# A three-layer graph network with a mixture-of-experts stage on one core: the first tiles of the next stage are put ahead of the last kept-back products

## The reference

```python
def _sage_layer(x, src, dst, Wl, bl, Wr, a):
    msg = x[src]
    agg = jax.ops.segment_sum(msg, dst, num_segments=n)
    deg = jax.ops.segment_sum(jnp.ones(...), dst, num_segments=n)
    agg = agg / jnp.maximum(deg, 1.0)[:, None]
    out = agg @ Wl + bl + x @ Wr
    return jnp.where(out >= 0, out, a * out)
...
x = x + three _sage_layers(_layernorm(x))
h = _layernorm(x); probs = softmax(h @ Wr + br); the two largest of 8 stay as cw
x = x + sum over e of cw[:, e] * (relu(h @ W1[e] + b1[e]) @ W2[e] + b2[e])
```

## Time and profile before

| | |
|---|---|
| median of 3 runs | 2694.34 us (2692.85 to 2696.75) |
| the profiled execution | 2695.04 us, its span 2693.4 us |
| PE busy | 2629.3 us, 98% of the span |
| VectorE, ScalarE, GpSimd busy | 1806.5, 1270.8, 992.5 us |
| mean granted clock of TensorE | 0.992 of full speed |

### The profile page before, as it was taken

The page is one execution under the profiler, slowest core; times in us unless marked ns, Lnnn a source line. Parts: engine busy times, 40 slices in busy tenths (PEclk is TensorE's granted clock), DMA queues, the critical chain, the costliest instruction groups (busy, mean ns, idle before and its releaser), DMA issues.

```text
span 2693.4 us, 39731 instructions
## 1 busy us (share of the span) xinstructions
PE 2629.3 (98%) x9195; PEld 1508.0 (56%) x9195; DVE 1806.5 (67%) x5090; ACT 1270.8 (47%) x2681; POOL 992.5 (37%) x1054
## 2 busy tenths in 40 slices
PE   7999999999899999999899999999899999999999
PEld 3444445554588855555488865555455555555554
DVE  5555555554799955555599965555477777777775
ACT  2222245554488855555288855555222222222222
POOL 2222255553344445554233335555222222222221
PEclk9999999999999999999999999999999999999999
DMA  4344378886255568887245558888422222222221
GB/s 133 133 133 132 118 224 271 264 273 224 88 164 164 164 201 269 273 263 259 90 164 164 164 181 268 268 272 264 148 85 86 82 83 90 85 82 83 89 85 48
DMA packets 200943, 446.57 MB, mean 166 GB/s; under 512 B 34383, under 2 KB 34695, under 8 KB 200836
## 3 DMA queue, kind: packets, MB, share of 16 engines
q0 software_dynamic: 64928, 207.55, 26.7%
q10 hardware_dynamic: 69168, 126.12, 12.8%
q1 hardware_dynamic: 66740, 111.54, 11.8%
HBM read 238.50 MB, written 207.11 MB: 165 GB/s over the span
## 4 chain that ended last, share of the span: by engine, by line
PE 95%; DMA 2%; DVE 1%; ACT 1%; issue 1%; SPq 0%; DVEq 0%; POOL 0%; ACTq 0%; POOLq 0%
PE psY L602 11%; PE psY L582 10%; PE psH L582 10%; PE psM L713 9%; PE psY L713 8%; PE psH L713 8%; PE psT L576 6%; PE psY L616 6%; PE psY L624 5%; PE psY L633 5%; PE psS L725 4%; PE psS L726 4%; PE psM L582 2%; PE psH L602 2%; PE psS L576 1%; PE psH L809 1%
## 5 line engine op out<-in xcount | busy, mean ns | idle before, releaser
L510 POOL DMA_INDIRECT rows<-y_rows,lists x471 | 487.3, 1035 | 473.9 <-PE psS L726 313.5
L1186 DVE TENSOR_TENSOR lows<-rows,highs 128x512 fp32r<-128x512 f32 x471 | 326.1, 692 | 374.5 <-ACT highs L842 341.4
L517 POOL DMA_INDIRECT rows<-sum_rows,nodeI x237 | 296.0, 1249 | 338.7 <-DVE rows L1194 305.2
L842 ACT ACTIVATE outs<-psS 128x512 f32<-128x512 f32 x471 | 279.6, 594 | 284.9 <-PE psS L726 251.3
L842 ACT ACTIVATE highs<-rows 128x512 fp32r<-128x512 f32 x471 | 294.6, 625 | 144.1 <-ACT outs L842 98.6
L725 PE MATMUL psS<-highs,sel 128*128 128x512 f32 x471 | 348.8, 740 | 7.3 <-ACT outs L842 7.3
L491 POOL TENSOR_TENSOR st<-st,small 128x1 f32<-128x1 f32 x158 | 90.0, 570 | 663.2 <-DVE st L1086 663.2
L602 PE MATMUL psY<-wy,res 128*128 128x512 f32 x632 | 287.0, 597 | 0.8 <-ACT res L842 0.8
L582 PE MATMUL psY<-wy,xTs 128*128 128x512 f32 x632 | 285.8, 595 | 0.0
L582 PE MATMUL psH<-wz,hTs 128*128 128x512 f32 x632 | 284.2, 592 | 0.7 <-ACT hTs L842 0.7
L713 PE MATMUL psM<-wz,res 128*128 128x512 f32 x544 | 255.4, 592 | 0.0
(11 more groups left out here) (166 smaller groups left out, 4108.9 us busy)
## 6 DMA issues: line engine op xcount, KB each, us to landing
sum_rows<-outs ACTq DMA_DIRECT2D x471, 256.0 KB
y_rows<-outs SPq DMA_DIRECT2D x237, 256.0 KB
rows<-in_x POOLq DMA_DIRECT2D x78, 256.0 KB, 2.9
outs<-in_x SPq DMA_DIRECT2D x78, 256.0 KB
out_rows<-res SPq DMA_DIRECT2D x78, 256.0 KB, 2.0
rows<-y_rows,lists POOLq DMA_INDIRECT x471
rows<-sum_rows,nodeI POOLq DMA_INDIRECT x237
wy<-in_L_gnn_Wl SPq DMA_DIRECT2D x3, 1024.0 KB, 7.2
```

The costliest lines, as they stand in the source:

```text
L510: pool.indirect_dma_start(out=rows[:, t % RING, :], out_offset=None, in_=y_d, in_offset=bass.IndirectOffsetOnAxis(ap=col(srcT, t), axis=0) ...
L517: pool.indirect_dma_start(out=rows[:, s, :], out_offset=None, in_=s_d, in_offset=bass.IndirectOffsetOnAxis(ap=col(nodeI, t), axis=0), boun ...
L842: act.activation(o, i_, ACT.Copy).then_inc(signal, 1)
L1186: dve.tensor_tensor(lows[:, t % RING, :], rows[:, t % RING, :], highs[:, g, :].bitcast(F32), ALU.subtract)\
```

## The change

At the first two changes of stage, PE transposes tiles 0 and 1 of the next layer between k6 and k7, and its wait for all `z_sb` before the second transpose is gone. VectorE makes `next_x` of tiles 0 and 1 behind `take_z` of k5, `bend` and `x_high` of tile 0 (`high_x`, cut out of `split_x`) behind that of k6, and `w_low` between `take_z` of k7 and of k8. ScalarE's first copy waits for `mend_add` (the mended sums added, which frees `psS`) in place of all `z_ps`. At the third, VectorE does both `ahead` calls of the expert stage behind `take_z` of k5, and then takes k6, k7 and k8. PE's list is not changed there. The wait of ScalarE's `norm` is changed in the same way. An unused helper (`edge_blocks`) is gone, and the layer loop of VectorE stands behind the definition of `experts`; line numbers move by this.

```diff
@@ dense (PE)
-                x_transpose(0, 0, k)
-                all_turns(pe, z_sb, k)
-                x_transpose(0, 1, k)
                 pe.wait_ge(high_parts, k)
@@ sum stage (PE)
-                for node in late[2:]:
+                for node in late[2:-2]:
+                    z_product(*node, l)
+                if l + 1 < LAYERS:
+                    x_transpose(0, 0, l + 1)
+                    x_transpose(0, 1, l + 1)
+                for node in late[-2:]:
                     z_product(*node, l)
@@ ScalarE, layers 1 and 2
-                    all_turns(act, z_ps, l)
+                    act.wait_ge(mend_add, 2 * l)
@@ ScalarE, experts
-            all_turns(act, z_ps, LAYERS)
-            act.wait_ge(mend_ps, 2 * LAYERS)
+            act.wait_ge(mend_add, 2 * LAYERS)
@@ split_x (VectorE)
+            def high_x(i, c, k):
+                t, s, n = at(i, c, 2)
+                dve.wait_ge(xT_kept[s], k * uses(s) + n + 1)
+                dve.wait_ge(hh_ps, (k - 1) * NT + t)
+                dve.tensor_scalar(x_high[:, :], kept(t), UNDER, None, ALU.mult).then_inc(xh_set, 1)
+
             def split_x(i, c, k):
                 t, s, n = at(i, c, 2)
                 used = (k - 1) * NT + t
-                dve.wait_ge(xT_kept[s], k * uses(s) + n + 1)
-                dve.wait_ge(hh_ps, used)
-                dve.tensor_scalar(x_high[:, :], kept(t), UNDER, None, ALU.mult).then_inc(xh_set, 1)
+                if not (isinstance(i, int) and i + c == 0):
+                    high_x(i, c, k)
@@ VectorE, end of a layer (the loop stands elsewhere now; only what differs)
-                for node in late[3:]:
-                    take_z(*node, l)
-                if l + 1 < LAYERS:
-                    split_low(l)
-                all_turns(dve, z_sb, l + 1)
-                if l + 1 < LAYERS:
-                    next_x(0, 0, l + 1)
-                    next_x(0, 1, l + 1)
-                    bend(0, 0, l + 1)
-                    each_split(dve, lambda i, c: split_x(i, c, l + 1))
-                else:
-                    dve.wait_ge(avec_in, 16)
...
-            for t in range(2):
-                experts(0, t - 2, numbered(t, AHEAD, done[0]), own=False)
-            done[0] += 2 * AHEAD
+                for node in late[3:-3]:
+                    take_z(*node, l)
+                if l + 1 < LAYERS:
+                    next_x(0, 0, l + 1)
+                    next_x(0, 1, l + 1)
+                    take_z(*late[-3], l)
+                    bend(0, 0, l + 1)
+                    high_x(0, 0, l + 1)
+                    take_z(*late[-2], l)
+                    split_low(l)
+                    take_z(*late[-1], l)
+                else:
+                    dve.wait_ge(avec_in, 16)
+                    for t in range(2):
+                        experts(0, t - 2, numbered(t, AHEAD, done[0]), own=False)
+                    done[0] += 2 * AHEAD
+                    for node in late[-3:]:
+                        take_z(*node, l)
+                all_turns(dve, z_sb, l + 1)
+                if l + 1 < LAYERS:
+                    each_split(dve, lambda i, c: split_x(i, c, l + 1))
```

More of the change, by code:

```diff
@@ L305, in each_four @@
             step(PAIRS, 0)
-        def edge_blocks(eng):
-            yield (0, 1), [(0, 0), (0, 1)]
-            yield (1, 0), [(0, 2), (0, 3)]
-            yield (1, 1), [(1, 0), (1, 1)]
-            for i in span(eng, 2, PAIRS):
-                yield (i, 0), [(i, -2), (i, -1)]
-                yield (i, 1), [(i, 0), (i, 1)]
-            yield (PAIRS, 0), [(PAIRS - 1, 2), (PAIRS - 1, 3), (PAIRS, 0)]
         def landed(t, l):
@@ L1409, in _, with take_edge @@
             AHEAD, OWN = 6, 11
-            for t in range(2):
-                experts(0, t - 2, numbered(t, AHEAD, done[0]), own=False)
-            done[0] += 2 * AHEAD
+            for l in range(LAYERS):
+                if l == 0:
+                    make_plan()
+                dve.wait_ge(bvec_in, 16 * (l + 1))
+                def take_edge(e):
+                    select(*e, l)
+                    low(*e, l)
+                take_z(0, 0, l)
+                take_z(0, 1, l)
+                take_edge((0, 0))
+                take_edge((0, 1))
+                for t in range(2, FIRST):
+                    take_z(t // 2, t % 2, l)
+                for nodes, edges in sum_blocks():
+                    for e in two_on(edges):
+                        take_edge(e)
+                    for node in nodes:
+                        take_z(*node, l)
+                late = late_nodes()
+                take_z(*late[0], l)
+                if l + 1 < LAYERS:
+                    split_high(l)
+                take_z(*late[1], l)
+                for b, r in BLOCKS:
+                    g = MEND_SLOT[b]
+                    dve.wait_ge(mend_g[b], 16 * (l + 1))
+                    dve.wait_ge(mend_ps, 2 * l + b + 1)
+                    dve.tensor_tensor(rows[0:r, g, :], rows[0:r, g, :], psS[b][0:r, :], ALU.add)\
+                       .then_inc(mend_add, 1)
+                take_z(*late[2], l)
+                if l + 1 < LAYERS:
+                    split_cross()
+                for node in late[3:-3]:
+                    take_z(*node, l)
+                if l + 1 < LAYERS:
+                    next_x(0, 0, l + 1)
[12 more added lines that the diff above has]
+                    for node in late[-3:]:
+                        take_z(*node, l)
+                all_turns(dve, z_sb, l + 1)
+                if l + 1 < LAYERS:
+                    each_split(dve, lambda i, c: split_x(i, c, l + 1))
```

32 lines of the change are left out of this document (removed).

## The result

| | before | after |
|---|---|---|
| median, 8 runs each, taken side by side | 2696.18 us (2692.85 to 2697.07) | 2686.88 us (2686.25 to 2688.88) |
| the profiled execution, its span | 2695.04 us, 2693.4 us | 2686.95 us, 2685.2 us |

The ratio is 0.9969, with a 95% interval of 0.9958 to 0.9980. The medians differ by 9.3 us, the two profiled spans by 8.2 us. The forecast was 6.3 us.

What follows compares the result with a forecast made beforehand. PE, busy for 98% of the span, bounds the kernel, so time comes only from its idle or low-clock stretches. 7.1 - 0.8 = 6.3 us off 2695.04 gives 2688.7, median 2688.0; range 2683.5 to 2692.5.

Steps and rivals of the forecast that it cites:

- Transposes ahead of k7 and k8: First two changes of stage: two transposes moved ahead of k7 win 3.5 and 3.6 us, sum 7.1, bounds 6.5 to 7.6.
- So no wait, with a margin of 1.2 and 0.8 us: First two changes of stage: gathers land 3.4 us after issue, so the moved transposes find their input with this margin.
- rival D: Gathers of tiles 0 and 1 land late, PE waits ahead of k7 and its clock falls: slower, 2699.1 or 2701.1; 6%.
- The clock at the first two changes: PE's clock falls again behind k8: booked 0, bounds +1.8 for each change of stage above and -1 below.
- rival B: The clock holds at the first two changes, with one PE wait of 3.6 us: adds 3.6, 2684.4 us; 13%.
- A new wait of 2.7 us: Third change: k8 on PE waits for `take_z` of k6 behind the `ahead` calls, starting at 1942.8 instead of 1940.12.
- The two chances in three: Third change: the wait ahead of k8 may let the clock fall under k8, half of 3.3 us, booked as 1.1 lost.
- `b1` opens the first `own` row 3.3 us sooner: Third change: `b1`, issued at 1947.15, lands 4.3 us later, so VectorE's first `own` row starts at 1951.5.
- I take 1953.8 as the start of L1335: 2.5 us sooner, bounds 1.8 and 3.3: Third change: VectorE's row needing tile 2's `x` rows starts 2.5 us sooner, transfers being through 6.7 us behind first issue.
- PE resumes on the low clock: Third change: PE stands still from about 1953 till 1959.2, then runs on the low clock: 2.2 us lost, bounds 1.2 to 3.0.
- The sum: All three changes of stage: 7.1 us won at the first two, 0.8 lost at the third, 6.3 us won.
- A: The forecast itself, over the whole kernel: 6.3 us won, median 2688.0 us; 60%.

Runs made afterwards that it cites:

- the first experiment: The changed kernel with its third part undone, `take_z` of k6 to k8 ahead of the `ahead` calls again: 2687.28 us, ratio 0.9965.

## Why the prediction was right

**Transposes ahead of k7 and k8.** Right in place and sign. The forecast was 18.6 us from k5 to the third transpose; it is 18.08 at both changes of stage. Three terms were a little too dear. Behind k5's start `w_low` came after 14.92 us, not 15.04, as eight transposes among the products cost 0.88 and not 1.0. The wait for `w_low` was 0.15, not 0.33. And `next_x` of tile 2 followed `take_z` of k8 after 0.72, so the 0.25 for its own `z_sb` was nothing. Together 4.1 won for each (22.14 and 22.18 before), not 3.5 and 3.6.

**"So no wait, with a margin of 1.2 and 0.8 us".** No wait was right, the margin was not. I took 3.4 us from the issue of a gather to its reader. It was 3.68 both times (686.05 to 689.73, 1303.29 to 1306.97). A transpose follows the start of its `next_x` after 0.85, and tile 1's begins 0.5 behind the start of the eight, at 691.34 and 1308.09. That leaves margins of about 0.8 and 0.3 us. The experiment one place earlier shows the other side of this edge: rival D's mechanism, a late `next_x` ahead of a transpose and a lower clock behind it, is real. Only part of the delay was the gathers' there, and by the profiles the two changes of stage lost 6.1 us.

**The clock at the first two changes.** I booked 0, with 1.8 each as the bound. In the profiled execution it fell at the second and not at the first, and the first gave 1.5 more (5.54 in place of 4.06). That was rival B in one of two places. Which way it goes isn't settled by the program: the idle time was 3.20 at both, and the profile of the first experiment has the low clock at both, with 25.20 and 26.37 us to the transpose of tile 4. Six profiles have this order and this idle time: the clock fell behind it in three of six at the first change and in six of six at the second. No row tells what decides it. So the 1.5 us are a chance of about one in two that came out well in this execution.

**"A new wait of 2.7 us" ahead of k8.** It is 2.34, and k8 starts 2.5 later behind k5 than before. The two chances in three that the clock falls under it (1.1 us) were not paid in the changed kernel's profile. They were in that of the moved `b1` wait, where k8 took 5.40: 1.7 us, as priced. Six kernels have this wait of 2.34 or 2.35, and the clock fell under k8 in that one alone, so the chance was put too high.

**`b1` opens the first `own` row 3.3 us sooner.** It did: 21.58 us behind k5, against 24.98 before, so 3.4.

**"I take 1953.8 as the start of L1335: 2.5 us sooner, bounds 1.8 and 3.3".** This is the step that failed. It was 1.3 us sooner (25.14 behind k5 instead of 26.45), outside my bounds. I had let the transfers be through 6.7 us behind the first issue, as in the kernel before; it took 7.88 (1937.42 to 1945.30). In the kernel before, nobody had waited for these rows, so 6.7 rested on a DMA share in a window and not on a reader. And it was another burst. First the `x` rows' issues in the kernel before (tile 2 at 1948.5, tile 3 at 1952.4), then those of tiles 2 and 3 in the changed kernel with the time to landing, and the same in the kernel that issues them first:

```profile
L370 SPq DMA_DIRECT2D outs<-in_x x2: 327/328/328, 1948.5 to 1952.4; - x2
...
outs<-in_x SPq DMA_DIRECT2D x2, 256.0 KB, 7.0
...
outs<-in_x SPq DMA_DIRECT2D x2, 256.0 KB, 2.6
```

Before, tile 2's rows went out 4.0 us behind `b1`, and tile 3's only when all was through. In the changed kernel both went out within 1.4 us of `b1`, so the burst held one tile's 256 KB more. At the 404 GB/s of the window from 1943 to 1944 these are an estimated 0.65 us of the 1.2 by which the landing was late; what the rest is stays open. The Trainium skill (DMA: Bandwidth & Descriptors, "Issuing engines are not separate DMA queues") says that all transfers share the same 16 engines. The trace fits: the same rows landed 7.0 us after their issue behind `b1` and `W2`, and 2.6 when nothing stood ahead of them. It doesn't separate shared engines from a place in one queue. By that rule I had 1954.5 as the late end, nearer to what came, 1955.0 on the same scale.

**"PE resumes on the low clock", 2.2 us.** It was 2.5: 11.78 us between the transposes of tiles 2 and 3, against 9.28. The granted clock was 0.50 in the window of 1951, and full in that of 1957. In the three other profiles with this order the same two transposes lay 12.8 to 13.4 us apart, so 2.5 is the mildest case. PE stood still for 8.0 us and not for 6, mostly because L1280 was late. The Trainium skill (TensorE: Matmul & The Clock Gate, "HAM oscillation") counts half of the throttled time as lost. Over the 5 to 6 us in which PE was at work at the low clock this gives an estimate of 2.5 to 3, as measured; over the whole low stretch, which had begun between 1945 and 1947 while PE stood still, it would give about 5.

**The sum.** 4.1 + 4.1 + 1.5 for the clock, and 1.1 - 2.5 = -1.4 at the third: 8.2 us in the profile, where I had 7.1 - 0.8 = 6.3. The error of 1.9 is 1.0 from the two mis-sized terms, 1.5 from the clock, and -0.6 from the third change. (In the chances, three quarters of A and all of B make 0.58, not 0.59.) So a total near the forecast is partly errors that cancel, and partly luck: the third change cost 1.4 in this profile, and up to 3.2 in others. The medians lie 9.3 apart. The last 1.1 is that the profiled execution of the kernel before was 1.1 faster than its median of 2696.18, within what single runs scatter.

**What was not seen.** I costed the third change as a trade of one wait against another. The experiments show it as three waits in series, each hiding the ones behind it: k8's input, `b1`, the `x` rows. With the `b1` wait alone taken away, the next one grew from 2.01 to 5.12. With all three gone, 8.7 us came free, nearly as much as the whole change had given. From k5 to the transpose of tile 3 it is 35.44 us, 7.1 less than in the changed kernel and 5.7 less than in the kernel before.

Two things stay open. What the third part costs in the presence of the first two: 1.4 us by the balance of the two profiles, between 0.6 and 3.2 by all profiles with one order or the other, and 2.2 on the kernel before, while the medians with it undone scatter too widely to tell. And loading `b1` into a buffer of its own, ahead of the last products, was not tried.

## What to carry to other kernels

Work can be moved ahead of the last products only as far as its inputs have landed and the engine that prepares them has got to them: read the landing from a row whose reader waited, since one place further turned 9 us won into nothing. Where several waits stand in series at a change of stage, removing one shows little or nothing, because most of it goes into the next one; list them all from the timeline and remove them in one kernel. A wait belongs to the first instruction that reads what it waits for, not to the head of the stage, though for `b1` this paid only once the waits around it were gone too.
